# Parts of q and k moved from SBUF to SBUF, and large transfers placed at other steps

## The chip, the cores and the metric

One core of a Trainium2 chip runs the kernel. The metric is the time of one execution on the device in microseconds (us), the median of several runs. One more execution is profiled; all rows below are from it. PE is TensorE, DVE is VectorE, ACT is ScalarE, POOL is GpSimd, SP is SyncE. The granted clock is the share of 2.4 GHz that PE is given; it is 1.00 or 0.50 (1.2 GHz) at any moment.

## The reference

`x` is 4 x 1024 x 128 (B = 4 batches). First comes a time-mixing block: layer norm, three mixed projections, a decayed scan along time, a gate, a projection and the residual. Then a chain of 6 nodes of attention, with 8 heads of 16 columns over 1024 positions:

```python
for c in range(NUM_NOD):
    q = ew[c, 0] * (nodes[in_q] @ We[eq] + be[eq])
    k = ew[c, 1] * (nodes[in_k] @ We[ek] + be[ek])
    v = ew[c, 2] * (nodes[in_v] @ We[ev] + be[ev])
    o = _mha(q, k, v, Wq[c], Wk[c], Wv[c], Wo[c])   # softmax(qh kh' / 4) vh, then wo
    nodes[c] = act_w[c] * o + q
```

and a last layer norm and residual. Nearly all the time is in the attention.

## The kernel before

A **unit** is one node of one batch: 24 units, numbered 0 to 23. A unit has 4 groups (two sets of four heads times two halves of the query positions), a group has 8 **steps** (128 key positions each), so a unit has 32 steps and the program 768. Every engine runs the same list of steps `s = 32 u + r`, written out by hand, in its own order; semaphores tie them. In a step PE makes four score matmuls (line 442, `scores`), four matmuls for the maxima of a group 14 steps ahead (line 462, `maxima`), and the product with v (line 488, `weighted`). ACT takes the exponentials (line 740). DVE reduces the maxima (line 990).

The scores subtract the row's maximum inside the matmul: `q_aug` and `k_aug` hold, for each parity of the heads, 48 rows of data (3 slots of 16) and 2 rows more, ones in `k_aug` and the negated maxima in `q_aug`. The 48 rows give float32 accuracy: q and k are split on POOL into a high part (a cast, line 1077) and a low part (a subtraction, line 1079), kept in `q_part` and `k_part` [128, 2, 1024]; slots of q take parts 0, 1, 0 and those of k parts 0, 0, 1. Parts have one partition for each of the 128 columns, `q_aug` has 16 partitions a slot with four pairs of heads behind each other, so the rows must change partition. Before, `store_q` and `store_k` (lines 236, 232) write the parts to `part_dram`, 1 MB each, and `load_aug` (line 254) loads them back: 4 loads for q and 4 for k, of 32 partitions (512 KB) or 16 (256 KB). All are issued by POOL. Buffers are two, by the unit's parity.

Where the work of the next unit (`nxt = u + 1`) and of the one before (`prev = u - 1`) stands, by r:
- 0, 1: q's head products (line 380), evicted by ACT (line 662), split on POOL; r = 1: store of q's parts, r = 4: loads of q.
- 4, 5: the same for k (lines 372, 654), store; r = 8: loads of k. POOL also loads `src` (line 268), the input of k's and v's products, at r = 0 and 8.
- 12 to 15: output products of `prev` (lines 399, 404), 24, 25: v (line 391). These and q's and k's heads share one PSUM bank, MISC.
- maxima of group G: at s % 8 == 1 DVE combines the halves, at 2 it casts and splits them (lines 999, 1004), at 3 PE turns them (line 469) and DVE copies them out (line 1012), at 4 SP moves them into `q_aug` with 4 DMAs (`move_max`, line 1217); the scores of group G begin at the next multiple of 8.
- denominators: SP moves the context of a group to `ctxT` and the denominators to DRAM (`move_ctx`, lines 1234, 1236), for the last group of `prev` at r = 1; at r = 3 it loads them spread over 128 partitions (line 1241), at r = 5 DVE inverts them (line 942), at r = 6 SP stores them (line 1245), waits for that, and broadcasts them to `rden_bc` (line 1251); at r = 11 POOL multiplies (`normalise`, line 1092), and PE's output product of r = 13 waits for it.

Engines other than PE don't wait for a step's beginning: POOL and SP go on as soon as their semaphores allow.

Of the kernel before, what the change touches and what calls it, by code (L numbers as in the profile page):

```python
# [11 lines left out]
P = 128  # L12
BANK = 512
NODES = 6
# [11 lines left out]


def ascending_runs(slots):
    runs = []
    for i, part in enumerate(slots):  # L30
        if runs and part == runs[-1][1] + runs[-1][2]:
            runs[-1][2] += 1
        else:
            runs.append([i, part, 1])
    return runs
# [8 lines left out]
def build(nc, x, time_decay, mix_k, mix_v, mix_r, Wk, Wv, Wr, Wo, ln_g, ln_b, ew, act_w, We, be,  # L44
# [22 lines left out]
    with ctx:  # L67
# [14 lines left out]
        part_dram = dram("part_dram", [2, 2, 2, P, S])  # L82
# [4 lines left out]
        with ExitStack() as first:  # L87
# [60 lines left out]
        d_time, d_weights, d_out, d_src, d_x2in, d_part_q, d_part_k, d_aug = sems(  # L148
            "d_time d_weights d_out d_src d_x2in d_part_q d_part_k d_aug")
# [17 lines left out]
        AUG_LOADS_K = len(ascending_runs(K_SLOTS))  # L167
        AUG_LOADS_Q = len(ascending_runs(Q_SLOTS))
        AUG_ALL = DMA * 2 * (AUG_LOADS_K + AUG_LOADS_Q)

# [29 lines left out]
        QH_AT, KH_AT, OUT_AT, TURN_AT, V_AT = (0, 1), (4, 5), (12, 13, 14, 15), (16, 17), (24, 25)  # L200
# [27 lines left out]
        def store_k(e, u):  # L228
            e.wait_ge(g_k, 2 * u + 2)
            if u >= 2:  # L230
                e.wait_ge(d_aug, AUG_ALL * (u - 1))
            e.dma_start(part_dram[u % 2, 1].rearrange("p r s -> r p s"), k_part[:, :, :]).then_inc(d_part_k, DMA)

        def store_q(e, u):
            e.wait_ge(g_q, 2 * u + 2)
            e.dma_start(part_dram[u % 2, 0].rearrange("p r s -> r p s"), q_part[:, :, :]).then_inc(d_part_q, DMA)

        def load_aug(e, u, side, parity):
            aug, slots = ((q_aug, Q_SLOTS), (k_aug, K_SLOTS))[side]
            if parity == 0:  # L240
                if side == 1:
                    e.wait_ge(d_part_k, DMA * (u + 1))
                else:
                    e.wait_ge(d_part_q, DMA * (u + 1))
                if u == 0 or side == 0:
                    if u == 0:
                        e.wait_ge(a_fold, NODES)
                    if u == 1:
                        e.wait_ge(p_mt2, EARLY)
                    if u >= 2:  # L250
                        e.wait_ge(p_st, HG * UC * (u - 1))
            first = parity * ROWS
            for slot, p, n in ascending_runs(slots):
                e.dma_start(aug[first + slot * DH:first + (slot + n) * DH, u % 2, :, :],  # L254
                            part_dram[u % 2, side, p:p + n].rearrange("p (d r o) s -> o (p d) r s", r=PAIRS, o=2)[parity]
                            ).then_inc(d_aug, DMA)
# [14 lines left out]
        def tensor_program(e):  # L271
# [175 lines left out]
            def maxima(m):  # L447
# [12 lines left out]
                if t == 0 and g == 0:  # L460
                    e.wait_ge(d_aug, AUG_ALL * (u + 1))
# [32 lines left out]
            def product_of(s):  # L494
# [6 lines left out]
                if 1 <= nxt < UNITS:  # L501
                    if r in QH_AT:
                        return lambda: head_q(nxt, r - QH_AT[0], MISC)
                    if r in KH_AT:
                        return lambda: head_k(nxt, r - KH_AT[0], MISC)
                    if r in V_AT:
                        return lambda: project_v(nxt, r - V_AT[0], MISC)
                if 0 <= prev < LAST:
# [80 lines left out]
        def scalar_program(e):  # L589
# [57 lines left out]
            def evict_head_k(u, hf):  # L647
                c, _ = divmod(u, B)
                e.wait_ge(p_kh, 2 * u + hf + 1)
                if u > 0:  # L650
                    e.wait_ge(d_part_k, DMA * u)
# [5 lines left out]
            def evict_head_q(u, hf):  # L657
                c, _ = divmod(u, B)
                e.wait_ge(p_qh, 2 * u + hf + 1)
                if u > 0:  # L660
                    e.wait_ge(d_part_q, DMA * u)
# [16 lines left out]
            def stages(s):  # L678
                u, r = divmod(s, UC)
                nxt, prev = u + 1, u - 1  # L680
                if 1 <= nxt < UNITS:
                    if r in QH_AT:
                        evict_head_q(nxt, r - QH_AT[0])
# [720 lines left out]
```

## Time and profile before

| | us |
|---|---|
| median of 3 runs | 2590.36 (2585.66 to 2595.50) |
| profiled execution | 2579.65 |
| its span, first to last instruction | 2577.8 |
| mean granted clock of PE | 0.93 |

The page's row of busy time gives each engine's union of busy stretches. A row of stretches gives, for each stretch asked for, its length and each engine's busy time in it with the number of instructions, the mean granted clock, the share in which the 16 DMA engines were busy, and GB/s. "Idle before" is the time that an engine stood before an instruction, with what ended it.

### The profile page before, as it was taken

What the parts mean: (1) busy time and instruction counts of PE and PEld (TensorE: products, weight loads), DVE (VectorE), ACT (ScalarE), POOL (GpSimd) and SP (SyncE); (2) the same over time, 40 slices, a digit from 0 to 9 for tenths busy, and PEclk for the clock granted to TensorE, in tenths of its full rate; (3) what the DMA queues carried; (4) which work ended last, traced back from release to release, by engine and by line L of the source; (5) the groups of instructions that cost most, each with busy time, mean ns of one, the idle gap of its engine ahead of it and who ended that gap; (6) DMA issues with size and microseconds to landing.
All of it is one profiled execution on the core that took longest, in us unless ns stands there. A gap on an engine that the chain in (4) does not pass through costs nothing.

```text
span 2577.8 us, 45901 instructions
## 1 busy us (share of the span) xinstructions
PE 2455.9 (95%) x17003; PEld 998.8 (39%) x17003; DVE 2162.4 (84%) x3951; ACT 1807.8 (70%) x3425; POOL 456.8 (18%) x546
## 2 busy tenths in 40 slices
PE   6489999999999999999999999999999999999997
PEld 3334334434434433433434334434434434433342
DVE  6478888979979988888878889888978989989894
ACT  3136667767767777777767778777777767777775
POOL 1221212012012022022021121121021121122201
PEclk8678989989989998999889999999989989999998
DMA  3412314154253254153252451452352341442401
GB/s 90 108 46 51 89 34 97 39 113 98 42 113 96 43 114 102 36 115 90 47 102 58 83 111 49 85 105 58 74 104 56 77 102 43 91 105 61 92 17 49
DMA packets 88222, 198.88 MB, mean 77 GB/s; under 512 B 21050, under 2 KB 38734, under 8 KB 87998
## 3 DMA queue, kind: packets, MB, share of 16 engines
q0 software_dynamic: 40320, 146.82, 27.0%
q1 hardware_dynamic: 47678, 49.12, 7.9%
q8 instruction: 135, 2.21, 0.4%
q14 instruction: 89, 0.73, 0.1%
HBM read 116.65 MB, written 64.42 MB: 70 GB/s over the span
## 4 chain that ended last, share of the span: by engine, by line
PE 75%; DMA 10%; DVE 10%; issue 2%; POOL 1%; SPq 1%; ACT 0%; POOLq 0%; DVEq 0%; ACTq 0%
PE bank L442 29%; PE bank L488 27%; PE bank L462 7%; DVE max_half L990 6%; DMA q_aug<-max_rows 5%; DMA rden_bc<-rden_dram 3%; PE bank L391 2%; PE bank L399 2%; PE bank L380 2%; PE bank L404 2%; DMA rden_dram<-rden_pack 1%; SPq L1217 1%; PE bank L303 1%; DMA k_aug<-part_dram 1%; PE bank L372 1%
## 5 line engine op out<-in xcount | busy, mean ns | idle before, releaser
L990 DVE TENSOR_REDUCE max_half<-bank 128x1 f32<-128x512 f32 x3072 | 1936.8, 684 | 324.6 <-PE bank L462 288.2
L740 ACT ACTIVATE e_ring<-bank 128x512 f32<-128x512 f32 x3072 | 1634.4, 601 | 604.2 <-PE bank L442 597.0
L462 PE MATMUL bank<-k_aug,q_aug 48*128 48x512 f32 x3072 | 1241.6, 477 | 41.4 <-DMA k_aug<-part_dram 22.4
L442 PE MATMUL bank<-q_aug,k_aug 50*128 50x512 f32 x3072 | 1181.5, 464 | 20.0 <-DMA q_aug<-max_rows 19.5
L488 PE MATMUL bank<-e_ring,v_aug 128*32 128x256 f32 (+1 forms) x9632 | 956.2, 470 | 0.6 <-ACT raw L751 0.4
L442 PEld LDWEIGHTS bank<-q_aug,k_aug 50*128 50x128 f32 x3072 | 535.7, 193 | 896.5 <-ACT e_ring L740 759.2
L462 PEld LDWEIGHTS bank<-k_aug,q_aug 48*128 48x128 f32 x3072 | 539.2, 193 | 131.8 <-DVE max_half L990 89.0
L488 PEld LDWEIGHTS bank<-e_ring,v_aug 128*32 128x32 f32 x9632 | 192.7, 109 | 334.6 <-issue 241.8
L268 POOL DMA_DIRECT2D src<-node_dram x40 | 23.6, 590 | 768.2 <-PE bank L391 765.8
L1077 POOL CAST q_part<-q_part 128x512 fp32r<-128x512 f32 x48 | 29.6, 617 | 467.2 <-ACT q_part L662 466.9
L1092 POOL TENSOR_TENSOR ctxT<-ctxT,rden_bc 128x1024 f32<-128x1024 f32 x23 | 54.4, 2363 | 174.3 <-DMA rden_bc<-rden_dram 174.1
L1055 POOL TENSOR_TENSOR rstd<-vareps,neg_half 128x4 f32<-128x4 f32 x24 | 25.3, 1056 | 284.4 <-DVE vareps L784 284.4
L254 POOL DMA_DIRECT2D k_aug<-part_dram x96 | 50.2, 529 | 125.6 <-DMA part_dram<-k_part 125.4
L751 ACT ACTIVATE raw<-bank 128x512 f32<-128x512 f32 x96 | 57.4, 598 | 18.1 <-PE bank L488 17.2
L254 POOL DMA_DIRECT2D q_aug<-part_dram x96 | 50.4, 532 | 93.0 <-DMA part_dram<-q_part 88.9
L1079 POOL TENSOR_TENSOR k_part<-k_part 128x512 f32<-128x512 f32 x48 | 61.2, 1274 | 4.0
L1079 POOL TENSOR_TENSOR q_part<-q_part 128x512 f32<-128x512 f32 x48 | 61.0, 1272 | 3.9
L399 PE MATMUL bank<-node_ring,w_edge_q 128*128 128x512 f32 x96 | 60.7, 717 | 0.0
L404 PE MATMUL bank<-ctxT,w_o 128*128 128x512 f32 x92 | 51.8, 645 | 4.4 <-POOL ctxT L1092 4.4
L380 PE MATMUL bank<-node_ring,w_q 128*128 128x512 f32 x96 | 55.6, 663 | 0.0
L372 PE MATMUL bank<-src,w_k_fold 128*128 128x512 f32 x80 | 49.8, 707 | 0.0
L391 PE MATMUL bank<-w_v_fold,src 128*128 128x128 f32 x320 | 46.3, 288 | 0.0
(184 smaller groups left out, 882.7 us busy)
## 6 DMA issues: line engine op xcount, KB each, us to landing
part_dram<-k_part POOLq DMA_DIRECT2D x24, 1024.0 KB, 6.8
part_dram<-q_part POOLq DMA_DIRECT2D x24, 1024.0 KB, 4.4
q_aug<-part_dram POOLq DMA_DIRECT2D x48, 512.0 KB, 8.6
k_aug<-part_dram POOLq DMA_DIRECT2D x48, 512.0 KB, 12.6
src<-node_dram POOLq DMA_DIRECT2D x40, 512.0 KB, 5.2
q_aug<-part_dram POOLq DMA_DIRECT2D x48, 256.0 KB, 9.7
k_aug<-part_dram POOLq DMA_DIRECT2D x48, 256.0 KB, 10.8
ctxT<-raw SPq DMA_DIRECT2D x384, 32.0 KB
```

Of the source, the lines that this page charges most:

```text
L254: e.dma_start(aug[first + slot * DH:first + (slot + n) * DH, u % 2, :, :], part_dram[u % 2, side, p:p + n].rearrange("p (d r o) s -> o (p ...
L372: e.matmul(bk[:, :], w_k_fold[:, c, :], source(u, hf), start=True, stop=True).then_inc(p_kh, 1)
L380: e.matmul(bk[:, :], w_q[:, c, :], node_ring[:, b, c % 2, half_of(hf)], start=True, stop=True).then_inc(p_qh, 1)
L391: done = e.matmul(bk[:, j * P:(j + 1) * P], data[:, j * P:(j + 1) * P], w_v_fold[:, c, :], start=True, stop=True)
L399: e.matmul(bk[:, :], w_edge_q[:, c, :], node_ring[:, b, c % 2, half_of(hf)], start=True, stop=False)
L404: e.matmul(bank[MISC][:, :], w_o[:, c, :], ctxT[:, half_of(hf)], start=False, stop=True).then_inc(p_o, 1)
L442: e.matmul(bank[i][:, :], k_aug[first:first + AUG, u % 2, h // 2, chunk * P:(chunk + 1) * P].bitcast(F32R), q_aug[first:first + AUG, u % 2 ...
L462: e.matmul(bank[i][:, :], q_aug[first:first + SPLIT, u % 2, h // 2, q0:q0 + P].bitcast(F32R), k_aug[first:first + SPLIT, u % 2, h // 2, ha ...
L488: done = e.matmul(bank[CTX_BANK][j * VW:(j + 1) * VW, columns], v_aug[:, u % 2, chunk, hg * HG + j, :], e_ring[:, (HG * z + j) % E_SLOTS, ...
L740: e.activation(e_ring[:, n % E_SLOTS, :], bank[i][:, :], ACT.Exp, scale=EXP_SCALE).then_inc(a_exp, 1)
L990: e.tensor_reduce(max_half[:, G % 2, row, kh:kh + 1], bank[MAX_BANKS[m % 3]][:, :], AX_X, ALU.max).then_inc(v_mx, 1)
L1079: signal(e.tensor_tensor(x, x, high, ALU.subtract), signal_to)
```

## The change

- `store_k`, `store_q`, `load_aug` and `part_dram` go. `move_parts` copies straight from `q_part` or `k_part` to `q_aug` or `k_aug`: for each parity and slot one DMA of 16 destination partitions, read from every second partition of the source, 256 KB, six for q and six for k, issued by POOL.
- q's head products, evictions and splits move from r = 0, 1 to r = 30, 31 of the unit before; q is moved at r = 1, k at r = 8.
- `src` is loaded at r = 26 of the unit before (from r = 0) and at r = 14 (from r = 8).
- The denominators are loaded at r = 4, inverted at r = 6, stored and broadcast at r = 7 (from 3, 5, 6).
- Before the first unit the moves come at z = 3, k first.

```diff
-        QH_AT, KH_AT, OUT_AT, TURN_AT, V_AT = (0, 1), (4, 5), (12, 13, 14, 15), (16, 17), (24, 25)
+        KH_AT, OUT_AT, TURN_AT, V_AT, QH_AT = (4, 5), (12, 13, 14, 15), (16, 17), (24, 25), (30, 31)
...
+        def move_parts(e, u, aug, part, slots, signal):
+
+            if u < 2:
+                e.wait_ge(a_fold, NODES)
+                if u == 1:
+                    e.wait_ge(p_mt2, EARLY)
+            else:
+                e.wait_ge(p_st, HG * UC * (u - 1))
+            for parity in range(2):
+                for slot, i in enumerate(slots):
+                    first = parity * ROWS + slot * DH
+                    e.dma_start(aug[first:first + DH, u % 2, :, :], part[parity:P:2, i, :]).then_inc(signal, DMA)
+
+        def move_q(e, u):
+            e.wait_ge(g_q, 2 * u + 2)
+            move_parts(e, u, q_aug, q_part, Q_SLOTS, d_q)
...
                 if t == 0 and g == 0:
-                    e.wait_ge(d_aug, AUG_ALL * (u + 1))
+                    e.wait_ge(d_q, DMA * Q_MOVES * (u + 1))
+                    e.wait_ge(d_k, DMA * K_MOVES * (u + 1))
...
-                    if half == 0 and r == 5:
+                    if half == 0 and r == 6:
                         e.wait_ge(d_den_in, DMA * (prev + 1))
...
+                if 1 <= nxt + 1 < UNITS and half == 1:
+                    if r == 26:
+                        load_source(e, nxt + 1, 0)
+                    if r in QH_AT:
+                        split_q(nxt + 1, r - QH_AT[0])
                 if 1 <= nxt < UNITS and half == 1:
-                    if r == 0:
-                        load_source(e, nxt, 0)
-                    if r in QH_AT:
-                        split_q(nxt, r - QH_AT[0])
-                    if r == QH_AT[-1]:
-                        store_q(e, nxt)
-                    if r == 4:
-                        for parity in range(2):
-                            load_aug(e, nxt, 0, parity)
+                    if r == 1:
+                        move_q(e, nxt)
                     if r in KH_AT:
                         split_k(nxt, r - KH_AT[0])
-                    if r == KH_AT[-1]:
-                        store_k(e, nxt)
                     if r == 8:
+                        move_k(e, nxt)
+                    if r == 14:
                         load_source(e, nxt, 1)
-                        for parity in range(2):
-                            load_aug(e, nxt, 1, parity)
...
-                        if r == 3:
+                        if r == 4:
                             load_den(prev)
-                        if r == 6:
+                        if r == 7:
                             spread_rden(prev)
```

## Rows read from the trace of the kernel before

**Rows 1.** The page, part 1: busy us, share of the span, instructions.

```profile
PE 2455.9 (95%) x17003; PEld 998.8 (39%) x17003; DVE 2162.4 (84%) x3951; ACT 1807.8 (70%) x3425; POOL 456.8 (18%) x546
```

**Rows 2.** Stretches: sums of groups 0 and 1 (units 2 to 22), three groups alone.

```profile
sum 563.74, PE 543.80 PEld 197.88 DVE 467.14 ACT 423.50 POOL 245.24; mean PE 25.90 PEld 9.42 DVE 22.24 ACT 20.17 POOL 11.68
...
632.46:656.49 24.03, 24.03 (x161) 9.01 (x161) 20.66 (x36) 18.31 (x35) 4.44 (x5) 1.00 0.80 130
...
1218.01:1250.41 32.40, 32.40 (x161) 10.88 (x162) 21.17 (x36) 18.85 (x35) 4.44 (x5) 0.68 0.57 97
...
sum 573.63, PE 567.43 PEld 202.77 DVE 442.14 ACT 389.46 POOL 93.44; mean PE 27.02 PEld 9.66 DVE 21.05 ACT 18.55 POOL 4.45
...
1250.41:1271.13 20.72, 20.72 (x190) 8.90 (x186) 19.84 (x36) 17.39 (x34) 0.00 (x0) 1.00 0.13 40
```

**Rows 3.** Stretches, steps 0, 3, 5, 7, 19, 31 of unit 10.

```profile
1191.62:1195.02 3.40, 3.40 (x23) 1.26 (x19) 3.01 (x5) 2.59 (x6) 0.00 (x0) 1.00 0.00 0
...
1200.88:1204.74 3.86, 3.84 (x22) 1.39 (x18) 3.86 (x8) 2.56 (x5) 0.75 (x1) 1.00 0.67 262
...
1208.13:1211.52 3.39, 3.39 (x23) 1.13 (x20) 2.82 (x5) 2.75 (x6) 1.88 (x2) 1.00 1.01 168
...
1213.99:1218.01 4.02, 2.70 (x29) 1.20 (x25) 3.06 (x5) 2.35 (x5) 1.32 (x2) 1.00 1.05 228
...
1257.99:1260.92 2.93, 2.93 (x22) 1.18 (x19) 2.93 (x6) 2.24 (x5) 0.00 (x0) 1.00 0.33 131
...
1290.95:1293.58 2.63, 2.63 (x28) 1.17 (x24) 2.63 (x5) 2.22 (x5) 0.00 (x0) 1.00 0.02 6
```

**Rows 4.** Who waited for whom: us in total, times, longest.

```profile
PE bank L462 <- DMA k_aug<-part_dram: 22.4, 1, 22.4
PE bank L442 <- DMA q_aug<-max_rows: 19.5, 15, 1.7
```

**Rows 5.** Order of time, PE: start, length; idle before and what ended it.

```profile
1218.01 0.50 PE L442 MATMUL bank<-q_aug,k_aug 50*128 50x512 f32 x1 [1.32 <-DMA q_aug<-max_rows]
```

**Rows 6.** Order of time, SP's issues in unit 10.

```profile
1205.22 2.67 SPq L1217 DMA_DIRECT2D q_aug<-max_rows  x4
...
1218.44 0.65 SPq L1251 DMA_DIRECT2D rden_bc<-rden_dram  x1
```

**Rows 7.** Order of time, POOL in unit 10.

```profile
1199.44 1.28 POOL L1079 TENSOR_TENSOR q_part<-q_part 128x512 f32<-128x512 f32 x1
...
1205.71 2.10 POOL L254 DMA_DIRECT2D q_aug<-part_dram  x4 [3.95 <-DMA part_dram<-q_part]
...
1229.61 2.36 POOL L1092 TENSOR_TENSOR ctxT<-ctxT,rden_bc 128x1024 f32<-128x1024 f32 x1 [6.37 <-DMA rden_bc<-rden_dram]
```

**Rows 8.** Line 254's landing, q then k loads of unit 10; stretches inside q's.

```profile
DMA to landing us min/median/max: 6.2/8.8/10.9
...
DMA to landing us min/median/max: 9.3/12.9/16.5
...
1207.00:1209.40 2.40, 2.40 (x17) 0.94 (x16) 1.58 (x4) 1.85 (x4) 1.64 (x4) 1.00 0.89 216
1210.00:1212.00 2.00, 2.00 (x15) 0.79 (x16) 1.59 (x3) 1.48 (x3) 0.57 (x2) 1.00 1.00 125
```

**Rows 9.** Order of time, DVE in unit 10.

```profile
1199.64 1.10 DVE L999 CAST max_part<-max_neg 128x16 fp32r<-128x16 f32 x1
...
1209.91 0.55 DVE L942 RECIPROCAL rden_pack<-den_pack 128x64 f32<-128x64 f32 x1
...
1227.97 0.17 DVE L999 CAST max_part<-max_neg 128x16 fp32r<-128x16 f32 x1
```

**Rows 10.** DMA issues: KB each, median us to landing; line 1245's landing.

```profile
src<-node_dram POOLq DMA_DIRECT2D x40, 512.0 KB, 5.2
den_pack<-den_dram SPq DMA_DIRECT2D x23, 32.0 KB, 1.7
...
DMA to landing us min/median/max: 1.4/7.9/8.8
```

More of the change, by code:

```diff
@@ L25 @@
 WKV_EPS = 1e-8
[L28 to L35, printed above, removed]
 def node_sources(c):
@@ L81, in build @@
         node_dram = dram("node_dram", [SPILLED + 1, B, P, S])
-        part_dram = dram("part_dram", [2, 2, 2, P, S])
         den_dram = dram("den_dram", [2, H, S])
@@ L146, in build @@
         g_k, g_q, g_norm, g_out = sems("g_k g_q g_norm g_out")
-        d_time, d_weights, d_out, d_src, d_x2in, d_part_q, d_part_k, d_aug = sems(
-            "d_time d_weights d_out d_src d_x2in d_part_q d_part_k d_aug")
+        d_time, d_weights, d_out, d_src, d_x2in, d_q, d_k = sems(
+            "d_time d_weights d_out d_src d_x2in d_q d_k")
         d_den_in, d_rden_out, d_rden_in, d_last_den = sems("d_den_in d_rden_out d_rden_in d_last_den")
@@ L166, in build @@
         WEIGHT_LOADS = 2 + 1 + 3 * NODES + 4 + 2
-        AUG_LOADS_K = len(ascending_runs(K_SLOTS))
-        AUG_LOADS_Q = len(ascending_runs(Q_SLOTS))
-        AUG_ALL = DMA * 2 * (AUG_LOADS_K + AUG_LOADS_Q)
+        Q_MOVES, K_MOVES = 2 * len(Q_SLOTS), 2 * len(K_SLOTS)
         def halves(t):
@@ L225, in build, with move_k @@
         where = {}
-        def store_k(e, u):
-            e.wait_ge(g_k, 2 * u + 2)
[L230 to L256, printed above, removed]
+        def move_parts(e, u, aug, part, slots, signal):
[12 more added lines that the diff above has]
+            move_parts(e, u, q_aug, q_part, Q_SLOTS, d_q)
+        def move_k(e, u):
+            e.wait_ge(g_k, 2 * u + 2)
+            move_parts(e, u, k_aug, k_part, K_SLOTS, d_k)
         def load_source(e, u, which):
@@ L501, in product_of @@
                 if 1 <= nxt < UNITS:
-                    if r in QH_AT:
-                        return lambda: head_q(nxt, r - QH_AT[0], MISC)
                     if r in KH_AT:
@@ L507, in product_of @@
                         return lambda: project_v(nxt, r - V_AT[0], MISC)
+                if 1 <= nxt + 1 < UNITS and r in QH_AT:
+                    return lambda: head_q(nxt + 1, r - QH_AT[0], MISC)
                 if 0 <= prev < LAST:
@@ L650, in evict_head_k @@
                 if u > 0:
-                    e.wait_ge(d_part_k, DMA * u)
+                    e.wait_ge(d_k, DMA * K_MOVES * u)
                 else:
@@ L660, in evict_head_q @@
                 if u > 0:
-                    e.wait_ge(d_part_q, DMA * u)
+                    e.wait_ge(d_q, DMA * Q_MOVES * u)
                 e.activation(q_part[:, 1, half_of(hf)], bank[where["qh", u, hf]][:, :], ACT.Identity,
@@ L681, in stages @@
                 if 1 <= nxt < UNITS:
-                    if r in QH_AT:
-                        evict_head_q(nxt, r - QH_AT[0])
                     if r in KH_AT:
                         evict_head_k(nxt, r - KH_AT[0])
+                if 1 <= nxt + 1 < UNITS and r in QH_AT:
+                    evict_head_q(nxt + 1, r - QH_AT[0])
                 if 0 <= prev < LAST:
@@ L1163, in gpsimd_program @@
                         split_k(0, hf)
-                    store_k(e, 0)
                     for hf in range(NHALF):
                         split_q(0, hf)
-                    store_q(e, 0)
-                if z == 4:
-                    for side in range(2):
-                        for parity in range(2):
-                            load_aug(e, 0, side, parity)
+                if z == 3:
+                    move_k(e, 0)
+                    move_q(e, 0)
             e.wait_ge(p_mt2, EARLY)
```

1 line of the change is left out of this document (removed).

## Prediction

> **What bounds the kernel now.** I read the page's busy times first, then the stretches, then the waits. PE is busy for 95% of the span, DVE for 84% [rows 1]: a gain must come from steps that are longer than their work, and stretches show which these are. A unit is 32 steps. I cut each of the 21 units from 412.34 to 2466.64 into four groups of eight steps (a step begins with its first score matmul). Unit 10 starts at 1191.62; times with + count from a unit's start.
>
> In group 2 of unit 10, which has no head or output product, DVE is busy for 19.84 of 20.72 us: it sets the pace there [rows 2]. The odd groups are 0 and 1. Group 1 takes 24.03 us in a unit with the full granted clock and 32.40 in unit 10, with a mean clock of 0.68; over the 21 units it sums to 573.63 where 21 x 24.03 would be 504.6 [rows 2]. Nine of the 21 have a clock under 1.00. So 69.0 us go to low clock and what starts it, 7.7 us each.
>
> Group 0 is read by steps [rows 3]. Steps with a product take 3.4 (0 and 5 stand for 1 and 4), others 2.47 (step 6, from 1211.52 to 1213.99) or 2.63 (step 31). Step 3 takes 3.86, DVE busy throughout; the like step 19 takes 2.93. Step 7 takes 4.02 although PE is busy for 2.70. Step 7 is PE waiting for the DMA of the maxima: 15 waits, 19.5 us, 1.32 us in unit 10 [rows 4, 5]. SP issued those moves at 1205.22, 13.6 us into the unit [rows 6], POOL issued the four q loads from 1205.71 on, the last at 1207.3, and the last of these lands 10.9 us after its issue, at 1218.2 [rows 7, 8], just as PE goes on at 1218.01: the small moves are through only with the last large one. The clock falls there too: 0.68 over 32.40 us is 20.7 us at 1.2 GHz, and they begin with the wait. Of the 15 waits eight are followed at once by low clock; seven, 0.97 to 1.30 us long, are not. Step 3's cause is a cast of DVE's, 1.10 us there and 0.17 in group 1: it starts at 1199.64, inside POOL's subtraction for q's second half (1199.44 to 1200.72) [rows 7, 9], and the turned maxima wait for it.
>
> **The change part by part.** *Q's heads* move from steps 0 and 1 to steps 30 and 31 of the unit before, with two evictions on ACT and four operations on POOL (idle there). A product makes a step of 2.47 or 2.63 one of 3.4 [rows 3], so group 0 loses 0.93 + 0.76 and group 3 gains as much, 1.69. That cancels. What stays: POOL's subtraction, which ends 5.7 us after its product's step starts (1200.72 less 1195.02), now ends at +2.3, three steps before the cast, and step 3 loses its 0.93.
>
> *The q moves* are issued at +2.6 instead of +14.1. Their length is the main unknown: no row has a large move from SBUF to SBUF. The loads land 6.2 to 10.9 us after issues that begin 1.6 us apart, so (10.9 + 1.6 - 6.2) / 3 = 2.1 us from one to the next; with 512 KB 216 GB/s flowed, with 256 KB on 16 partitions 125, so the half-size load takes as long [rows 8]. Each new move has 256 KB on 16 partitions. Bounds are 1.2 us (256 KB at 216 GB/s) and 2.9 (the k loads, 9.3 to 16.5 us with the broadcast beside them [rows 8]). I take 2.1, the row of the same shape. With 6.2 - 2.4 = 3.8 us before the first data, six are through at +2.6 + 3.8 + 12.6 = +19.0. The maxima are now issued at +11.0 (+13.6 less 0.93, 0.76, 0.93) and needed at the end of group 0: 26.39 (1218.01 less 1191.62) - 0.93 - 0.76 - 0.93 - 1.40 = +22.4. That holds up to 2.67 us a piece. Step 7 becomes 2.62: -1.40. POOL issues 12 pieces of 0.53 us instead of 8 loads and 2 stores; nobody waits for that.
>
> The Trainium skill, page "SBUF — State Buffer", section "Door 1: The DMA port swizzle", speaks against this cut: 16 adjoining partitions reach 4 of 16 ports, measured at 104 GB/s. By it a piece takes an estimated 2.5 us and six are through at +21.5, the maxima still in time, the denominators (below) not; rival A is that case.
>
> *The reciprocals.* SP loads the denominators at step 4 instead of 3, DVE inverts at step 6 instead of 5. Step 5 has a product and leaves DVE idle for 0.57 us even with the reciprocal (2.82 busy of 3.39) [rows 3]; from step 6 on DVE sets the pace, so its 0.55 us [rows 9] shows: I take +0.5, bounds 0 and 0.55. The load also waits for the five context moves, which SP issues at about +3.6 to +6.6, now amid q's pieces. If each gets its turn after one piece, the fifth is through at +16.9 and the load lands 1.7 us later [rows 10], +18.6; DVE comes to the reciprocal at +17.3 (step 6) + 1.8 (1209.91 less 1208.13) = +19.1. In time by half a microsecond. If they wait for all six, it lands at +20.7 and DVE waits 1.6 us. The trace doesn't settle it (four small moves behind four loads fit both); I take turns, since nothing in the code orders SP's queue behind POOL's.
>
> *The k moves* are issued at +19.9 (5.7 us after step 5 starts, at +13.9) without a store before them, and are through at +36.3 alone; the k loads needed 18.0 us from first issue to last landing beside the broadcast, q's 12.5 [rows 7, 8], so +41.8 with it. Step 12's maxima are due at +46.4 (22.4 + 24.03). The reciprocals' store is issued at +19.9 as well and takes 1.4 us on an empty queue, 7.9 in the median [rows 10]; I take 1.4, as k's first data come over a microsecond after their issue. The broadcast took 11.1 us (1218.44 to 1229.61) and POOL's product 2.36 [rows 6, 7]: 21.3 + 11.1 + 2.4 = +34.8. PE's output product needs it at step 13: 22.4 + 24.03 - 3 x 3.39 = +36.3, and some 0.9 us into that step, +37.2. Slack 2.4 us.
>
> *The source loads* have no one waiting for 20 us; 5.2 us to land [rows 10] if that cover were gone. *Before the first unit* PE waits 22.4 us for k_aug [rows 4]. Issue comes about 3 us earlier without the stores' waits, but 12 pieces replace 8 loads of equal length: I take +1, bounds -3 and +8.
>
> **Sum** over the 21 units. Group 0 from 563.74 [rows 2] to 21 x (22.4 + 0.5) = 480.9: -82.8. Group 1 to 504.6: -69.0. Group 3, 20 times +1.69: +33.8. New low-clock stretches from short waits at step 13: +10. Prologue +1. Together -107.0; the span 2577.8 becomes 2470.8, with the 1.85 us outside it 2472.6. The profiled execution (2579.65) lies 10.7 us under the median of the runs, 2590.36; low clock that comes and goes may be why, and there will be less of it, so I add only 2.4: 2475.
>
> **The rivals.**
> A, half of it. The denominators are 1 to 1.6 us late at step 6 (pieces of 2.5 us, or no turns). For: the margin is half a microsecond. Against: 125 GB/s. Price 21 x 1.2 = 25, and low clock in a third of the units, 7 x 7.7 = 54, less the 10 counted: 2544.
> B, low clock has another cause and stays. For: seven waits without it. Against: eight times it begins at the wait. Then 0.93 + 1.40 - 0.5 a unit remain: 2590 - 38 = 2552.
> C, slower than before: the reciprocals' store queues behind k's pieces on the DMA engines and takes the 7.9 us that it takes behind q's loads now. Then the product on POOL ends at 27.8 + 11.1 + 2.4 = +41.3, PE waits 4.1 us at step 13 of every unit and loses the clock: 11.8 us against a gain of 107/21 = 5.1, so 2590 + 21 x 6.7 = 2731. It decides from a store of 5.1 us on, when the wait reaches 1.3 us. For: both are issued at +19.9. Against: k's data start later than the store's.
> D, the pieces take 2.9 us: denominators and maxima 3 us late and low clock every unit, 10.7 - 5.1 = 5.6 a unit, 2708. For: the row of k. Against: that row has the broadcast beside it, q's pieces don't.
>
> **How the numbers follow.** Forecast 0.60, A 0.17, B 0.07, C 0.09, D 0.07. Low end: no new low clock (-10), a free reciprocal (-10.5), a quick prologue (-4) and the profiled level (-5): 2445. High end takes in A and B and leaves out C and D: 2555. A measurement tells about 0.5%, 13 us, from no change. Faster: forecast, A, B and a mild C, 0.86; same 0.03; slower 0.11.
>
> **What would show it.** Step 3 near 2.9 and step 7 near 2.6, the cast at 0.17 in group 0, no wait of the scores for max_rows; group 0 near 22.9, group 1 near 24.03 at full clock, group 3 near 24.1. It is wrong if DVE's reciprocal waits for den_pack, if PE's output product waits for POOL, or if pieces land over 2.6 us apart.

## The result, and the profile after

| | us |
|---|---|
| before, on the same chips, median | 2578.36 (2549.72 to 2595.50) |
| after, median | 2614.89 (2585.73 to 2643.47) |
| ratio after / before | 1.013, 95% interval 1.009 to 1.017 |
| after, span of the profiled execution | 2583.9 |
| its mean granted clock | 0.938 |

The change made the kernel 1.3% slower; the forecast was 2475. Ratios, here and below, leave out executions more than 1.5% above the quickest of the same kernel, so they can differ by up to a per cent from the quotient of the medians. The profiled execution of after is the quickest of its runs, some 29 us under their median, so its trace shows rather too little of the loss than too much.

The stretches answer to [rows 2]: sums of groups 0, 1 and 3 over units 2 to 22 (columns: length, busy time of each engine, mean of one stretch).

```profile
sum 511.53, PE 493.79 PEld 189.78 DVE 435.87 ACT 395.24 POOL 245.04; mean PE 23.51 PEld 9.04 DVE 20.76 ACT 18.82 POOL 11.67
...
sum 600.43, PE 567.65 PEld 202.99 DVE 438.95 ACT 389.17 POOL 61.44; mean PE 27.03 PEld 9.67 DVE 20.90 ACT 18.53 POOL 2.93
...
sum 505.22, PE 505.22 PEld 219.57 DVE 465.91 ACT 388.33 POOL 49.53; mean PE 24.06 PEld 10.46 DVE 22.19 ACT 18.49 POOL 2.36
```

The forecast had 480.9, 504.6 and 505.5. Group 3 is right to 0.3 us. Group 0 gained 52.2 of the 82.8 us that it was to gain. Group 1 should have lost 69.0 us and grew by 26.8; there PE is busy for 567.65 of 600.43 us, so part of the surplus is idle time and part is PE at a lower clock. The steps of unit 10, which starts at 1186.96, show where (steps 3, 7, 13 and 14; the clock stands third from the end). They answer to [rows 3].

```profile
1194.54:1197.46 2.92, 2.92 (x21) 1.18 (x17) 2.92 (x6) 2.25 (x5) 0.00 (x0) 1.00 1.03 132
...
1206.71:1210.41 3.70, 3.33 (x30) 1.28 (x26) 3.70 (x7) 2.34 (x5) 3.01 (x6) 1.00 0.76 126
...
1224.30:1233.09 8.79, 5.56 (x22) 1.47 (x18) 2.58 (x4) 2.75 (x5) 2.90 (x2) 0.67 0.25 73
1233.09:1236.92 3.83, 3.83 (x22) 1.47 (x19) 2.58 (x4) 2.17 (x4) 0.00 (x0) 0.87 0.00 0
```

Step 3 is as forecast. Step 7 has DVE busy throughout and is 1.1 us over the forecast 2.62. Step 13, 3.39 us of work, takes 8.79: PE stands for 3.2 us and then runs in part at 1.2 GHz. The table of waits says for whom (us in total, times, longest); it answers to [rows 4].

```profile
PEld bank L382 <- POOL ctxT L1071: 38.8, 14, 4.1
PE bank L382 <- POOL ctxT L1071: 32.6, 14, 3.7
DVE rden_pack L921 <- DMA den_pack<-den_dram: 21.8, 20, 1.9
```

The scores' wait for `max_rows` (19.5 us in 15 times before) is in the table no more. Two waits have come: DVE's reciprocal at step 6 waits for the denominators in 20 units, 1.1 us each, and PE's output product at step 13 waits for POOL's product on the context in 14 units, 2.3 us each. In order of time, unit 10, for SP, DVE, POOL and PE (start, length, what; in brackets idle before and what ended it), answering to [rows 6, 7 and 9]:

```profile
1190.24 3.93 SPq L1206 DMA_DIRECT2D ctxT<-raw  x4
1194.22 1.39 SPq L1208 DMA_DIRECT2D den_dram<-raw  x1
1197.96 2.67 SPq L1189 DMA_DIRECT2D q_aug<-max_rows  x4
1204.94 0.32 SPq L1213 DMA_DIRECT2D den_pack<-den_dram  x1
1207.25 0.33 SPq L1217 DMA_DIRECT2D rden_dram<-rden_pack  x1
1211.68 0.66 SPq L1223 DMA_DIRECT2D rden_bc<-rden_dram  x1
...
1206.67 0.55 DVE L921 RECIPROCAL rden_pack<-den_pack 128x64 f32<-128x64 f32 x1 [0.58 <-DMA den_pack<-den_dram]
...
1226.11 2.34 POOL L1071 TENSOR_TENSOR ctxT<-ctxT,rden_bc 128x1024 f32<-128x1024 f32 x1 [16.25 <-DMA rden_bc<-rden_dram]
...
1228.50 2.08 PE L382 MATMUL bank<-ctxT,w_o 128*128 128x512 f32 x2 [3.23 <-POOL ctxT L1071]
```

Between the end of SP's context moves (+8.7) and its load of the denominators (+18.0) stands only the issue of the maxima: the load waits for the landing of the context. q's six pieces landed at +6.8, 10.1, 12.8, 14.3, 16.7 and 17.7; the context at +17.9, the maxima at +18.4. So all that SP issued from +3.3 to +13.7 is through just after the last piece. Beside k's burst (issued +19.9 to +22.9, landed +24.2 to +35.4) it is otherwise: the reciprocals' store, issued at +20.3 behind the first piece alone, is through at +24.7, half a microsecond after that piece. The broadcast, issued at +24.7 behind all six, is through at +39.1. The store's row (issue to landing) answers to [rows 10]:

```profile
DMA to landing us min/median/max: 1.4/7.6/9.7
```

Seven of the stores of units 2 to 22 are issued at +20.3 to +20.5 and land at +24.7 or +24.8, eleven at +20.6 to +21.4 and land beside the third piece (+28.6 to +29.1), two at +21.6 and land at +31.3, behind the fourth piece; one, issued at +19.6 ahead of the burst, takes 1.4 us. None waits for the end of the burst. In each of these units POOL begins its product at +38.9 to +39.7, whatever the store took.

The packets of the DMA queues show the same order (queue: packets, MB, share of the 16 engines; q0 has POOL's issues, q1 has SP's). The first two rows are unit 10 of this kernel from +3.3 to +11.7, the third is the same stretch of e4 below, where all six pieces are issued before SP's first move and q1 has no row at all, the fourth is this kernel from +24.7 to +32.7, the 8 us behind the issue of the broadcast:

```profile
q0 software_dynamic: 322, 1.08, 90.8%
q1 hardware_dynamic: 64, 0.07, 7.6%
...
q0 software_dynamic: 311, 1.02, 104.7%
...
q0 software_dynamic: 287, 0.96, 104.1%
```

Where SP's moves are issued between the pieces, they run between the pieces: the packets of the four context moves of unit 10 begin at +5.2 to +6.9, +8.1 to +10.2, +11.8 to +13.9 and +14.8 to +17.2. Where they are issued behind all pieces, their first packet begins at +11.8 (e4), and the broadcast's at +32.7.

Low clock begins at step 7 in twelve units and at step 13 in ten, in the steps of these two waits.

### The profile page after: what moved, and what is told of

The parts are those of the page before. It is cut to its first block, busy times and chain, and to the rows that moved or that the text cites. A ratio compares the mean times of both kernels' runs of the same rounds, so it can differ in the third digit from the quotient of the medians.

```text
span 2583.9 us, 45966 instructions
## 1 busy us (share of the span) xinstructions
PE 2442.5 (95%) x17011; PEld 994.6 (38%) x17011; DVE 2140.5 (83%) x3951; ACT 1803.1 (70%) x3425; POOL 463.6 (18%) x594
## 3 DMA queue, kind: packets, MB, share of 16 engines
q0 software_dynamic: 28800, 96.49, 24.7%
HBM read 41.15 MB, written 14.09 MB: 21 GB/s over the span
## 4 chain that ended last, share of the span: by engine, by line
PE 71%; issue 10%; DVE 7%; DMA 4%; POOL 4%; SPq 1%; ACT 1%; POOLq 0%; ACTq 0%; DVEq 0%
PE bank L420 27%; PE bank L467 25%; PE bank L441 7%; DVE max_half L969 4%; DMA den_dram<-raw 3%; PE bank L382 2%; PE bank L358 2%; PE bank L369 2%; POOL k_aug L226 2%; PE bank L377 1%; PE bank L350 1%; POOL ctxT L1071 1%; SPq L1206 1%; PE bank L281 1%; DMA q_aug<-q_part 1%
## 5 line engine op out<-in xcount | busy, mean ns | idle before, releaser
L420 PE MATMUL bank<-q_aug,k_aug 50*128 50x512 f32 x3072 | 1169.5, 460 | 0.6 <-ACT e_ring L719 0.2
L420 PEld LDWEIGHTS bank<-q_aug,k_aug 50*128 50x128 f32 x3072 | 529.4, 191 | 863.8 <-ACT e_ring L719 759.2
L382 PE MATMUL bank<-ctxT,w_o 128*128 128x512 f32 x92 | 59.7, 735 | 32.6 <-POOL ctxT L1071 32.6
L226 POOL DMA_DIRECT2D q_aug<-q_part x144 | 73.0, 514 | 9.1 <-POOL q_part L1058 6.2
L226 POOL DMA_DIRECT2D k_aug<-k_part x144 | 72.6, 511 | 8.9 <-POOL k_part L1058 6.2
L1056 POOL CAST k_part<-k_part 128x512 fp32r<-128x512 f32 x48 | 29.3, 610 | 234.6 <-ACT k_part L633 234.4
L730 ACT ACTIVATE raw<-bank 128x512 f32<-128x512 f32 x96 | 57.4, 598 | 18.6 <-PE bank L467 17.5
L641 ACT ACTIVATE q_part<-bank,col 128x512 f32<-128x512 f32 x48 | 32.7, 682 | 20.4 <-PE bank L358 20.4
```

The source lines that it names most:

```text
L226: e.dma_start(aug[first:first + DH, u % 2, :, :], part[parity:P:2, i, :]).then_inc(signal, DMA)
L382: e.matmul(bank[MISC][:, :], w_o[:, c, :], ctxT[:, half_of(hf)], start=False, stop=True).then_inc(p_o, 1)
L420: e.matmul(bank[i][:, :], k_aug[first:first + AUG, u % 2, h // 2, chunk * P:(chunk + 1) * P].bitcast(F32R), q_aug[first:first + AUG, u % 2 ...
L1056: step(e.tensor_copy(high.bitcast(F32R), x))
```

## The experiments

Two theories at first. The first: low clock and lost time in groups 0 and 1 follow from these two waits, and the waits from small transfers that stand beside a burst. The other: the low clock comes from something else, the traffic or the load on the chip, and will stay or move when a wait goes. Ratios are to the kernel before, run beside each kernel on the same chip, with a 95% interval; G0 and G1 are the sums of groups 0 and 1 over units 2 to 22 of the profiled execution.

| | ratio | interval | G0 | G1 |
|---|---|---|---|---|
| before | 1 | | 563.74 | 573.63 |
| after | 1.013 | 1.009-1.017 | 511.53 | 600.43 |
| e1 direct only | 1.030 | 1.024-1.037 | 569.94 | 626.40 |
| e2 placement only | 1.035 | 1.027-1.042 | 536.38 | 639.90 |
| e3 product first | 1.001 | 0.997-1.006 | 506.04 | 569.75 |
| e4 heads at 28 | 1.019 | 1.012-1.026 | 479.80 | 628.06 |
| e5 both | 0.984 | 0.977-0.991 | 480.02 | 571.83 |
| e6 k's pieces, then product | **0.973** | 0.967-0.978 | 479.71 | 505.36 |
| e7 q in halves | 1.068 | 1.058-1.079 | 478.31 | 738.42 |
| e8 = e6 + hold of DVE | 1.014 | 1.004-1.023 | 510.65 | 608.13 |
| e9 = e6, q's heads late | 0.998 | 0.994-1.003 | 505.10 | 568.89 |
| e10 = e6 through DRAM | **0.970** | 0.962-0.979 | 483.94 | 508.00 |

### The two halves of the change, each alone

**e1_direct_only** keeps the steps of before and moves the parts directly (from the kernel before; k's store and loads are replaced in the same way).

```diff
                     if r == QH_AT[-1]:
-                        store_q(e, nxt)
-                    if r == 4:
-                        for parity in range(2):
-                            load_aug(e, nxt, 0, parity)
+                        move_q(e, nxt)
```

> The kernel before with the direct moves alone: q's heads stay at steps 0 and 1, the denominators at steps 3, 5, 6; q's six pieces are issued when the split is done (about +9.7 us from the unit's start), k's at about +22.5. Theory T (what sets the time is when a burst of large pieces ends against who needs a small transfer behind it; a burst of six pieces takes 15.2 us from first issue to last landing in the changed kernel): q through at about +25, just when the maxima are needed, so the waits for max_rows shrink to 0 to 0.5 us; the denominators load early and free, DVE does not wait; the broadcast runs beside k's pieces and takes about 14 us as in the changed kernel, so PE may wait up to 2 us at step 13. Ratio to before 0.985 to 1.00. Rival R (the direct moves are what costs, wherever they stand): 1.01 or more.

Measured: 1.030. The number expected by the first theory was missed. Its waits:

```profile
PEld bank L392 <- POOL ctxT L1081: 49.5, 14, 7.9
PE bank L392 <- POOL ctxT L1081: 43.3, 11, 7.5
PE bank L430 <- DMA q_aug<-max_rows: 19.0, 12, 2.1
```

q's pieces are issued at +9.4 and through at +24.6, the maxima with them (+24.8 to +26.5); k's pieces follow at once (+22.5) and the broadcast stands beside them: POOL's product begins at +43.5 in unit 10 (+36.1 to +46.5 in all), against +38.0 before. The direct way took the store's place, not the collision's.

**e2_placement_only** takes the steps of the change and goes through DRAM (from the kernel after; k likewise).

```diff
                     if r == 1:
-                        move_q(e, nxt)
+                        store_q(e, nxt)
+                        for parity in range(2):
+                            load_aug(e, nxt, 0, parity)
```

> The changed kernel with its new places, but through DRAM: at each place the store of the parts and behind it the four loads. Theory T: store from +2.6, loads from about +7, through at about +19.5 to 20, so the context moves and the denominators are later than in the changed kernel (den_pack lands at +21 or later, DVE waits 1.5 to 2.5 us at step 6), step 3 stays at 2.9, no wait for max_rows; ratio 1.01 to 1.03, as bad as the changed kernel or worse. Rival R (the direct moves are what costs): 0.96 to 0.98.

Measured: 1.035, with DVE's wait for the denominators at its worst, 1.9 us on average:

```profile
DVE rden_pack L942 <- DMA den_pack<-den_dram: 40.2, 21, 4.6
```

Here the context lands early (+9.7 in unit 10; q's loads are issued from +7.9 on), but the load of the denominators, issued at +13.8 behind q's four loads, takes 7.0 us in the median instead of 1.7 and lands at +20.8, as the last of them does (+20.6).

Neither half pays alone, and together they lose 1.3%: what the halves share is what stands beside a burst.

### The two waits, each taken away

**e3_norm_first.** The change, but POOL waits for the broadcast and multiplies before it issues k's pieces.

```diff
-                    if r == 8:
+                    if r == 8 and prev < 0:
                         move_k(e, nxt)
...
-                    if half == 0 and r == 11:
+                    if half == 0 and r == 8:
                         normalise(prev)
+                        if nxt < UNITS:
+                            move_k(e, nxt)
```

> The changed kernel with POOL's order turned: normalise of the unit before stands at step 8 ahead of the k moves, so that k's pieces start after the broadcast has landed. Theory T: the reciprocals' store lands about 2 us after its issue, the broadcast about 6 us later, near +28.5, the product ends near +31, k's pieces are through near +46; PE's wait for POOL at step 13 (32.6 us in 14 waits) goes to 0 and the low-clock stretches that begin at step 13 go too; DVE's wait for den_pack at step 6 (21.8 us) stays. Group 1 falls from 600 to about 540 us over the 21 units; ratio 0.975 to 0.99. Rival L (low clock comes whatever the waits are): at most the 32.6 us, ratio 1.00 to 1.01.

Measured: 1.001. The broadcast, alone now, takes 6.7 us from issue to POOL's product instead of 14.4, and no wait for the context is left. DVE's wait is (20.0 us, 20 times), and low clock now begins at step 7 in eleven of the units 2 to 22, and hardly elsewhere in groups 0 and 1: with one wait gone more of it hung on the other. The trace shows a third cost, new in this run: POOL's product now begins at +28.8 in the median and lies over DVE's cast of the maxima near +30, which takes 0.87 to 1.23 us in ten units instead of 0.17. As a number this fell to the other theory; e5 and e6 show why that doesn't bear it out.

**e4_heads28.** The change, with q's heads, evictions and splits at steps 28 and 29, so that POOL issues q's pieces at +0.1 instead of +2.6.

```diff
-                if 1 <= nxt + 1 < UNITS and r in QH_AT:
+                if 1 <= nxt + 1 < UNITS and r in qh_at(nxt + 1):   # (28, 29); unit 3: (30, 31)
```

> The changed kernel with one thing moved: the product, eviction and split of q's heads stand at steps 28 and 29 (in unit 3 at 30 and 31), so that q's six pieces are issued at +0.1 to +3.1 us of the unit instead of +2.6 to +5.6; k's pieces and the normalising stay where the change has them. Theory T (the end of q's burst sets when the context's rows and the denominators land): the burst ends at +15.5 instead of +17.8, the context lands at about +17 instead of +18.2, and VectorE's wait of about 1 us for the denominators is gone in nearly all units, and with it the low clock from step 7 on. The store of the reciprocals still stands beside k's pieces at about +20, so waits at step 13 and their low clock stay in some ten units: ratio to the kernel before 0.990 to 1.003. Rival L (q's place alone makes the whole gain, the order around the normalising gives nothing): 0.978 to 0.988, with no wait at step 13.

Measured: 1.019, outside what was expected, though DVE's wait did go (1.3 us, 2 times) and G0 fell to 479.80. The waits at step 13 did not stay in ten units, they came in all:

```profile
PE bank L385 <- POOL ctxT L1074: 73.0, 22, 4.9
```

The reciprocals' store is through in 1.4 us here, and the broadcast is issued at +21.1 instead of +24.7; yet POOL's product begins at +38.7 in unit 10, with k's last piece at +41.2 instead of +35.4. An earlier broadcast takes its share from k's pieces and is through hardly earlier than in after (+38.7 against +39.1). And since group 0 is shorter, PE comes to step 13 earlier and waits in each unit. So the store was never the lever: the two together, 1.5 MB of k and the broadcast, end when their sum is through.

**e7_q_halves.** Three of q's pieces at step 1, the other three at step 8 ahead of k's.

```diff
                     if r == 1:
-                        move_q(e, nxt)
+                        move_q(e, nxt, (0,))
...
                     if r == 8:
+                        move_q(e, nxt, (1,))
                         move_k(e, nxt)
```

> The changed kernel with one thing moved: of q's six pieces three are issued at step 1 as before and the other three at step 8, right ahead of k's six. Theory T (small moves issued beside a burst of pieces land when the burst ends): the first burst ends at about +12 to +13 us instead of +17.8 and the context lands at about +13 to +14 instead of +18.2, the load of the denominators follows at once, VectorE has no wait for them, the store of the reciprocals lands before the second burst, and the waits at step 13 go too: ratio to the kernel before 0.965 to 0.990 (the upper end if GpSimd's product comes to lie on VectorE's cast at +29). Rival (SyncE's moves are slow by themselves, some 10 us whatever is beside them): the context still lands at about +17 to +18, VectorE still waits, ratio 1.00 to 1.02.

Measured: 1.068, the far side of what was expected, and the run that tells most. SP in unit 10, which starts at 1227.6, then POOL and PE:

```profile
1230.84 3.33 SPq L1207 DMA_DIRECT2D ctxT<-raw  x4
1234.21 0.55 SPq L1209 DMA_DIRECT2D den_dram<-raw  x1
1238.54 2.67 SPq L1190 DMA_DIRECT2D q_aug<-max_rows  x4
1241.31 0.34 SPq L1214 DMA_DIRECT2D den_pack<-den_dram  x1
...
1270.50 2.34 POOL L1071 TENSOR_TENSOR ctxT<-ctxT,rden_bc 128x1024 f32<-128x1024 f32 x1 [18.91 <-DMA rden_bc<-rden_dram]
...
1272.90 2.08 PE L382 MATMUL bank<-ctxT,w_o 128*128 128x512 f32 x2 [7.69 <-POOL ctxT L1071]
```

The first burst is through at +11.7 and the context, issued at +3.3 to +7.2 as ever, at +12.0. With six pieces it was +17.7 and +17.9. The theory that SP's moves are slow by themselves is refuted. But the other three pieces lengthen the second burst: the broadcast, issued at +21.1 behind four of its nine pieces, ends at +43.0, while the last piece lands at +50.5. PE waits 180.5 us in 21 times and G1 grows to 738.42. The expectation left out that the broadcast stands beside nine pieces now.

**e5_both.** e3 and e4 together (its expectation calls e3 the run before).

> The order of the run before, and q's heads, evictions and splits at steps 28 and 29 instead of 30 and 31 (in unit 3 they stay at 30 and 31), so that q's six pieces are issued at about +0.5 instead of +2.6 us. Theory T: they are through at about +15.7, den_pack lands at about +17.4, before DVE's reciprocal at +19.1: its wait goes to 0, step 7 falls from 3.99 to 2.6 to 3.1, and no low clock begins at step 7. Both waits gone: ratio 0.955 to 0.97, near the 2475 us of the forecast. Rival L: 0.99 to 1.00.

Measured: 0.984, between the two expectations. Both waits are gone, but for 1.0 us of DVE's in two units, and G0 is 480.02. But nine of the units 2 to 22 have low clock from step 11 on. Two stretches of unit 11, and DVE's cast there (in order of time):

```profile
1295.08:1300.17 5.09, 4.22 (x22) 1.39 (x19) 5.09 (x10) 2.57 (x5) 4.22 (x8) 0.92 0.69 105
1300.17:1306.29 6.12, 6.12 (x24) 1.82 (x20) 2.66 (x5) 2.17 (x4) 0.00 (x0) 0.51 1.07 123
...
1293.85 1.94 DVE L981 CAST max_part<-max_neg 128x16 fp32r<-128x16 f32 x1
```

The first is step 11, the second step 12. POOL's product runs from 1293.39 to 1295.76 over the cast, which takes 1.94 us there and 0.17 in other groups: the conflict of [rows 9] again, made anew by the move of the product from +39 to +28. In 20 of the 21 units the cast takes 0.74 us or more, and in each of them it ends 0.03 or 0.04 us after POOL's product does.

**e6_k_first** is e5 with k's six issues (3.0 us of POOL) between the wait and the product.

```diff
                     if half == 0 and r == 8:
-                        normalise(prev)
+                        e.wait_ge(d_rden_in, DMA * (prev + 1))
                         if nxt < UNITS:
                             move_k(e, nxt)
+                        normalise(prev)
```

> As e5_both, but at step 8 GpSimd first waits for the spread reciprocals, then issues k's six pieces (3.0 us), and multiplies the context after that: the product lies at about +31 to +33.4 us of the unit and no more over VectorE's cast of the maxima at +29. Theory T (in e5_both that cast took 1.1 us and more instead of 0.16 beside GpSimd's product, TensorE waited at step 11, and low clock followed in ten units): step 11 back to 3.4 us without waits, the second groups of units 2 to 22 at about 24.6 us each at full clock, ratio to the kernel before 0.962 to 0.972. Rival (the low clock has another cause and moves to another step): 0.978 to 0.990 with as many low stretches as e5_both.

Measured: 0.973, 2469.45 us: faster than both kernels. Its slowest execution took 2480.76 us, the quickest of before beside it 2520.75. G0 479.71 and G1 505.36 beside the 480.9 and 504.6 of the forecast. Unit 10 (starts 1142.4) for SP, POOL and DVE, and the sum of group 1:

```profile
1163.46 0.66 SPq L1229 DMA_DIRECT2D rden_bc<-rden_dram  x1
...
1170.07 3.02 POOL L229 DMA_DIRECT2D k_aug<-k_part  x6 [8.09 <-DMA rden_bc<-rden_dram]
1173.10 2.38 POOL L1074 TENSOR_TENSOR ctxT<-ctxT,rden_bc 128x1024 f32<-128x1024 f32 x1
...
1171.51 0.17 DVE L981 CAST max_part<-max_neg 128x16 fp32r<-128x16 f32 x1
...
sum 505.36, PE 505.27 PEld 189.38 DVE 441.41 ACT 387.60 POOL 124.29; mean PE 24.06 PEld 9.02 DVE 21.02 ACT 18.46 POOL 5.92
```

The broadcast ends 6.6 us after its issue, the cast is at 0.17, and no stretch of low clock is left in groups 0 and 1 of units 2 to 22. The theory that the low clock would move elsewhere falls for these groups. Later in these units low clock is left: it begins at step 19 or 20 of units 21 and 22, behind a wait of PE for DVE of 0.45 us; before has the same wait and low clock there.

### The clock, and the way through DRAM

**e8_hold.** e6, with DVE held at step 6 by arithmetic.

```diff
+                        for _ in range(2):
+                            step(e.reciprocal(rden_pack[:, :], den_pack[:, :]))
+                            after()
                         e.reciprocal(rden_pack[:, :], den_pack[:, :]).then_inc(v_rec, 1)
```

> As e6_k_first, but at step 6 VectorE takes the reciprocals three times in a row instead of once, which gives the same values: it is held for some 1.1 to 1.3 us more there, with every transfer where e6_k_first has it. Theory T (a hold of VectorE of about 1 us at step 6 makes the maxima late, TensorE waits, and its clock then falls to 1.2 GHz for a while in many units, with no transfer to blame): step 7 at about 3.9 us, waits of some 1.1 us in all units, low clock from step 7 or 8 in 8 to 12 of the units 2 to 22, ratio to the kernel before 0.995 to 1.008 as for e3_norm_first, where the transfers made the hold. Rival (the low clock needs more than the wait; the hold costs its own 1.1 to 1.3 us in each of 21 units): ratio 0.980 to 0.986 and hardly a low stretch.

Measured: 1.014, slightly above what was expected. Step 7 takes 4.20 us in the median at full clock instead of 3.02, which is 1.18 x 21 = 24.8 us; G0 and G1 grow by 133.7 us. The other 109 us are low clock, begun at step 7 or 8 in 14 of the 21 units and again at step 11 in six. q's burst and the load of the denominators stand where e6 has them, so a late DVE does it, with no transfer to blame. What hangs on the reciprocals comes later, though: the broadcast is issued at +22.3 instead of +21.1, and POOL's product begins at +32.2 instead of +30.7 in unit 10. In five of the six units with a second low stretch the first one had moved DVE's cast to +31.7, under this product, and the cast took 2.65 to 2.98 us. So the 109 us are the price of the hold with this knock-on in it, not of the wait alone. It isn't certain each time: step 7 of unit 10 here took 4.20 us and PE kept its full clock.

```profile
1217.34:1221.54 4.20, 3.32 (x28) 1.28 (x25) 4.17 (x8) 2.34 (x5) 0.00 (x0) 1.00 0.11 20
1221.54:1224.02 2.48, 2.48 (x30) 1.04 (x26) 2.26 (x5) 2.01 (x5) 0.00 (x0) 1.00 0.48 135
```

**e9_k_first_late_q.** e6 with q's heads back at 30 and 31: the changed kernel, mended at POOL's product alone.

> As e6_k_first, but with the heads of q back at steps 30 and 31, where the change has them: it differs from the changed kernel only in that k's pieces and the product on the context both come behind the wait for the spread reciprocals, in this order. Theory T (q's burst, 2.6 us later, makes the denominators land about 1 us too late for step 6, in all units): VectorE waits some 1.0 us about 20 times, step 7 at about 3.9 us, low clock from step 7 in 8 to 12 units, no waits at steps 11 and 13; ratio to the kernel before 0.990 to 1.003. Rival (q's place counts for little once k's pieces are out of the way): 0.973 to 0.982.

Measured: 0.998, DVE waits 19.4 us in 20 times, low clock begins at step 7 in ten units. The cast lies under POOL's product in four (1.33 to 3.03 us). With that in it, the 2.6 us by which q's pieces go earlier are worth some 2.5%.

**e10_k_first_dram.** e6's places, but with the stores and loads of before; k's loads come behind POOL's product, at step 10. The edit against e6, at k's place:

```diff
                     if half == 0 and r == 8:
                         e.wait_ge(d_rden_in, DMA * (prev + 1))
                         if nxt < UNITS:
-                            move_k(e, nxt)
+                            store_k(e, nxt)
+                    if half == 0 and r == 10:
+                        e.wait_ge(v_cmb, (s + LOOKAHEAD - 1) // NCH + 1)
                         normalise(prev)
+                        if nxt < UNITS:
+                            for parity in range(2):
+                                load_aug(e, nxt, 1, parity)
```

> The placement of e6_k_first with the way of before: q and k go through DRAM again (one store and four loads each), q's store and loads at step 1 with its heads at steps 28 and 29, k's store behind the wait for the spread reciprocals, then the product on the context (it waits for VectorE's split of the maxima in step 10), then k's loads. Theory T (what counts is that nobody's small moves or the broadcast stand beside a burst; the direct route is not needed for that): groups 0 and 1 near the 22.8 and 24.1 us of e6_k_first in most units, ratio to the kernel before 0.970 to 0.985. Rival (the direct route itself carries the gain: store and loads take longer than the pieces, the maxima or the denominators come late, TensorE waits and low clock follows): DVE waits for den_pack or TensorE for the maxima or for the context, ratio 1.00 to 1.03.

Measured: 0.970, not to be told from e6. Here 116.65 MB are read from HBM and 64.42 written, with e6 41.15 and 14.09, and the time is the same:

```profile
HBM read 116.65 MB, written 64.42 MB: 73 GB/s over the span
```

So the direct way, the larger half of the diff, is worth nothing that these runs can tell; the order of the transfers is worth all of it. Whether the direct way leaves room for something else wasn't tried.

## Why the prediction was wrong, point by point

**Right.** The cast's conflict: 0.16 us in group 0 (1193.31), step 3 at 2.92. The maxima: needed at +22.4, through at +18.4, no wait. The pieces: issued at +2.6 and (17.7 - 6.8) / 5 = 2.2 us apart, where 2.1 was forecast; 123 GB/s flowed in the burst:

```profile
1193.00:1204.00 11.00, 11.00 (x73) 3.91 (x71) 10.00 (x19) 8.76 (x18) 1.88 (x2) 1.00 0.97 123
```

The Trainium skill, "SBUF — State Buffer", section "Door 1: The DMA port swizzle", with its 104 GB/s, gives an estimated end of the burst at +21.5; it ended at +17.7, so the rule's direction holds (16 partitions don't get the 216 GB/s of [rows 8]) and its size, an estimate of 2.5 us a piece against 2.2 measured, is some 15% too slow here. Step 6's reciprocal: +0.5 taken, 22.77 us of group 0 in e6 where 22.4 + 0.5 was forecast. The heads: group 3 505.22 for 505.5. That low clock follows waits, against rival B: e6 and e8. The sum itself: with hardly a wait, e6 has 985.07 us in groups 0 and 1, the forecast 985.5, and 2469.45 us in all for 2475. The total is partly luck. Low clock in units 21 and 22 puts groups 2 and 3 of e6 some 12 us over what was forecast for them and so stands in the place of the 10 us for step 13. And before ran in 2563.70 us beside e6, not in the 2590.36 that the forecast starts from: as a ratio, 0.973 (0.967 to 0.978) is less of a gain than 2475 / 2590 = 0.956.

**The first step that failed: "if each gets its turn after one piece".** I had written both outcomes down, found that the rows fit both, and took turns "since nothing in the code orders SP's queue behind POOL's". No order in the code is needed; the order of issue was enough. SP's moves do get turns among the pieces, but a turn takes some 3.2 us (first packets at +5.2, +8.1, +11.8 and +14.8), not the 2.1 of one piece, and the fifth move is issued at +7.3, behind the last piece (+5.1), so it comes through behind all six: +17.9 instead of +16.9. e7, with three pieces ahead, has the context at +12.0 where they end at +11.7; e4, with all six issued before SP's first move, at +17.0 where they end at +15.7. So the denominators landed at +19.7 instead of +18.6, and DVE, which came to them at +19.1 as forecast, waited. [Rows 8] had shown it: the maxima came through only with the last large load, and I had read that row so in the first part. This is rival A, 1.1 us instead of its 1.2.

**The second: the broadcast's 11.1 us, and 1.4 for the store.** The forecast took both as durations of their own, and the slack of 2.4 us came from that. The store took 7.6 in the median (rival C said 7.9), for the order of issue again: by the time it was issued one to four of k's pieces stood ahead of it. And PE's output product began 41.5 us into unit 10, where C had POOL's product end at +41.3. But C had the mechanism by the wrong end: it hung all on the store. e4's store took 1.4 us, as the forecast said and for the reason that it gave, and POOL's product still began at +38.7. What counts is k's burst plus the broadcast: k's pieces alone need 15.3 us from first issue to last landing (e5, +30.1 to +45.4), the broadcast alone 6.6; begun together at +19.9 to +21.1 they are through at +39 to +41. C's chance was 0.09, argued down with a reason (k's data start later) that holds for the store and not for the broadcast, which I had put next to the row of before without asking what stood beside it there.

**The third: +10 us for new low clock.** In groups 0 and 1 after has 126.5 us more than the forecast's 985.5. The waits themselves are 21 x 0.97 (3.99 us of step 7 in the median at full clock, 3.02 in e6) = 20.4 and 32.6 at step 13. The other 73.5 are what is left for low clock, seven times what was put down; e8 has 109 for a hold of 24.8. So the low clock behind the waits costs 1.4 times their length in this execution of after and 4.4 times in e8. In e9 G0 and G1 are 1073.99, 88.9 us over e6's 985.07; step 7 takes 3.79 us in the median at full clock, so the waits are 21 x 0.77 = 16.2 us and the rest is 4.5 times that. The figures of e8 and e9 have the late cast of some units in them.

**The range** left C out (and D). It took A and C as separate cases, while both are one mechanism, short transfers behind the pieces that were issued ahead of them. With its two places at once, the chance of slower should have been that of the fifth move coming late, which by my own words was open.

Left open: why a wait of the same length leads to low clock in one unit and not in the next (e8, 14 of 21; 0.45 us is enough in units 21 and 22); why a move waits for pieces of another queue that were issued ahead of it (the rows show the order, not its reason); and how the 29 us between the profiled execution of after and its median are spread.

## What to carry to other kernels

Price a transfer by what was issued ahead of it, also on another engine's queue. Here a small move came through behind the pieces issued before it: early when that was one piece, with the end of the burst when it was all of them. Two bursts that overlapped ended when their sum was through. So let bulk copies with slack wait for the short transfers on the chain (here k's pieces behind the broadcast, and q's burst 2.6 us earlier), and then look at what the moved operations now lie beside on the other engines. A wait of PE of about a microsecond in each period is to be priced with the clock that it can cost, here 1.4 to 4.5 times its own length on top.

## What the runs showed of the hardware

- Four moves of 32 KB and one of 8 KB on SP's queue beside a burst on POOL's queue: issued at +3.3 to +8.7, landed at +12.0, +17.0 and +17.9 with bursts that end at +11.7, +15.7 and +17.7 (unit 10 of e7, e4 and after).
- A store of 32 KB issued inside a burst of six pieces lands 4.3, 8 or 9.7 us later, behind the first, beside the third or behind the fourth piece, by about what was issued ahead of it (after, units 2 to 22); alone it takes 1.4.
- A broadcast of 128 x 1024 floats takes 6.6 us alone, 14.4 beside what is left of six pieces, 17.6 beside all six and 21.9 beside nine, in unit 10 of e6, after, e4 and e7. Its first packet begins 1.4 us after the issue in e6 and 8.0 us after it in after.
- 256 KB from SBUF to SBUF on 16 destination partitions: one each 2.2 us, 123 GB/s in the burst, like the 125 of the 16-partition load from DRAM [rows 8].
- POOL's product of 128 x 1024 over DVE's cast of 128 x 16 makes the cast 1.13 us in the median and up to 2.12 (e5, 20 of 21 units) instead of 0.17; the cast ends with the product.
- Some 126 MB more through HBM (116.65 and 64.42 MB against 41.15 and 14.09) cost nothing that can be measured, once they are placed well.
